# Rests of q and k of batches 3 to 5 subtracted on GpSimd instead of VectorE

## The reference, cut to what matters

```python
xn = layernorm(x)                                  # x is (8, 256, 128)
Q = rope(heads(xn, Wq)); K = rope(heads(xn, Wk)); V = heads(xn, Wv)     # 16 heads of 8
def attend(q, k):
    s = (q @ k.T + 0.1 * (q*q) @ (k*k).T) / sqrt(8)
    s = where(causal, s, -1e9)
    return softmax(s) @ V
out1 = attend(Q, K); out2 = attend(rotate_half(Q), rotate_half(K))      # equal scores
out = 0.5 * (out1 + out2) + 0.05 * (out1 * out2) * gate_w
x = x + out @ Wo.T
x = x + ffn0(layernorm(x)); x = x + attention1(layernorm(x)); x = x + ffn1(layernorm(x))
```

## Time and profile before

| | us |
|---|---|
| median of 3 runs | 329.7 |
| lowest and highest run | 328.73 and 331.28 |
| the profiled execution | 328.89 |
| its span in the profile | 326.9 |

### The profile page before, as it was taken

The page is one execution under the profiler, slowest core; times in us unless marked ns, Lnnn a source line. Parts: engine busy times, 40 slices in busy tenths (PEclk is TensorE's granted clock), DMA queues, the critical chain, the costliest instruction groups (busy, mean ns, idle before and its releaser), DMA issues.

```text
span 326.9 us, 8438 instructions
## 1 busy us (share of the span) xinstructions
PE 292.8 (90%) x2852; PEld 208.5 (64%) x2852; DVE 252.1 (77%) x1000; ACT 216.8 (66%) x494; POOL 176.5 (54%) x406
## 2 busy tenths in 40 slices
PE   7749779698999899999999999999999999999946
PEld 4526456466667676767776676766666665655625
DVE  7877979777878877677768677679798989895453
ACT  7661675566477768586767768597778777676711
POOL 5641674876774877777687614435453627170210
PEclk9976999999999999999999999999999999999996
DMA  6976214311213122221201110010211110100000
GB/s 198 323 169 156 65 54 113 115 49 39 80 49 117 52 65 66 52 82 38 71 23 53 36 58 27 24 59 27 69 31 60 41 42 28 42 4 19 18 8 24
DMA packets 23178, 21.59 MB, mean 66 GB/s; under 512 B 2944, under 2 KB 20096, under 8 KB 23136
## 3 DMA queue, kind: packets, MB, share of 16 engines
q1 hardware_dynamic: 23136, 21.05, 22.2%
HBM read 13.18 MB, written 7.34 MB: 63 GB/s over the span
## 4 chain that ended last, share of the span: by engine, by line
PE 55%; DVE 22%; POOL 9%; issue 7%; ACT 6%; POOLq 0%; ACTq 0%; DVEq 0%
PE bank L978 12%; DVE NM L757 7%; PE bank L1008 5%; PE bank L952 5%; PE bank L1021 5%; PE bank L928 3%; PE bank L929 3%; POOL XN L430 2%; PE bank L1067 2%; PE bank L956 2%; PE bank L926 2%; PE bank L889 2%; PE bank L1053 2%; ACT PB L590 2%; PE bank L875 2%
## 5 line engine op out<-in xcount | busy, mean ns | idle before, releaser
L590 ACT ACTIVATE PB<-bank 128x384 f32<-128x384 f32 (+1 forms) x256 | 134.8, 545 | 56.6 <-PE bank L954 31.9
L757 DVE TENSOR_REDUCE NM<-bank 128x2 f32<-128x512 f32 x128 | 83.9, 684 | 22.6 <-PE bank L929 22.2
L952 PE MATMUL bank<-QS,KS 128*128 128x256 f16 x256 | 69.8, 274 | 2.1 <-ACT PB L590 1.4
L978 PE MATMUL bank<-PB,VP 128*32 128x256 f32 (+1 forms) x1024 | 61.7, 358 | 2.5 <-POOL PB L469 1.7
L752 DVE CUSTOM_DVE_ANT_0 JUNK<-bank,MSF 128x128 bf16<-128x128 f32 x128 | 36.4, 285 | 24.5 <-PE bank L926 24.0
L754 DVE CUSTOM_DVE_ANT_0 JUNK<-bank,MSF 128x256 bf16<-128x256 f32 x128 | 53.7, 419 | 0.0
L978 PEld LDWEIGHTS bank<-PB,VP 128*32 128x32 f32 x1024 | 26.7, 109 | 25.6 <-issue 9.3
L469 POOL TENSOR_SCALAR_AFFINE_SELECT PB<-PB 128x512 f32<-128x512 f32 x64 | 41.1, 643 | 0.0
L926 PE MATMUL bank<-KS,QS 96*128 96x256 f16 x128 | 36.1, 285 | 0.0
L928 PE MATMUL bank<-KS,QS 96*128 96x256 f16 x128 | 35.2, 275 | 0.4
L929 PE MATMUL bank<-KS,QS 96*128 96x256 f16 x128 | 34.6, 271 | 0.0
(11 more groups left out here) (101 smaller groups left out, 608.1 us busy)
## 6 DMA issues: line engine op xcount, KB each, us to landing
scr<-PR SPq DMA_DIRECT2D x16, 256.0 KB, 2.8
QS<-scr SPq DMA_DIRECT2D x16, 128.0 KB, 2.6
QS<-scr SPq DMA_DIRECT2D x32, 64.0 KB, 2.8
KS<-scr SPq DMA_DIRECT2D x32, 64.0 KB, 2.8
KS<-scr SPq DMA_DIRECT2D x16, 128.0 KB, 3.0
scr<-PR SPq DMA_DIRECT2D x16, 128.0 KB, 1.9
out_x<-xs SPq DMA_DIRECT2D x8, 128.0 KB, 1.9
W<-in_w SPq DMA_DIRECT2D x1, 576.0 KB, 6.2
```

What stands on the lines that cost most here:

```text
L590: act.activation(PB[:, s % RING, 0:n], scored(i, s)[:, 0:n], ACT.Exp).then_inc(s_e, 1)
L757: dve.tensor_reduce(m[:, s, 0:2], o[:, :].rearrange("q (n k) -> q n k", n=2), AX.X, ALU.max, negate=True).then_inc(s_mx, 1)
L952: pe.matmul(o[:, 0:S], k[:, 0:P], q[:, :], start=True, stop=True)
L978: ins = pe.matmul(o, v, pr, start=(g % 2 == 0 and kt == 0), stop=True, skip_group_check=True)
```

## The change

The two `low` subtractions of batches 3, 4 and 5 move from DVE to POOL. They keep their slots. On each engine the tables are followed in the same way, so the place within the slot follows from the place of the code in the engine's loop: on POOL the slot begins with the `cut` (odd slots), goes on with the vectors of the other steps and the value spread (`spread_v`, slot 8), and the new `low_pool` comes behind these. No semaphore is added or removed: `low_pool` waits for `high` as `low` did and counts up the same semaphore.

```diff
+POOL_LOW = (3, 4, 5)
...
+            def low_pool(b, n):
+
+                p = b % 2
+                pool.wait_ge(s_hi, 2 * b + n + 1)
+                pool.tensor_tensor(PR[p][:, n, 2:4], QR[p][:, n], PR[p][:, n, 0:2], ALU.subtract).then_inc(s_lo, 1)
...
                         for n, step in enumerate(("rot_q", "rot_k")):
                             if a[step] == H * i + s:
                                 rotate(b, n)
+                        if a["lo"] == H * i + s and b in POOL_LOW:
+                            for n in range(2):
+                                low_pool(b, n)
...
-                        if a["lo"] == H * i + s:
+                        if a["lo"] == H * i + s and b not in POOL_LOW:
                             for n in range(2):
                                 low(b, n)
```

## The result

| | kernel before | changed kernel |
|---|---|---|
| median | 330.52 us (20 runs) | 328.12 us (20 runs) |
| lowest and highest | 327.67 to 331.72 | 326.51 to 330.09 |
| ratio, with 95% interval | | 0.9938 (0.9915 to 0.9962) |
| profiled execution, its span | 328.89, 326.9 | 329.68, 328.0 |

The ratio compares the fast runs alone, so it is not exactly the quotient of the medians. The changed kernel is faster by about 2 us; the interval leaves 0.8 to 2.8. The two profiled executions say the opposite: the changed kernel's is 0.8 us longer. So the first thing to learn is how far one profiled execution speaks for its kernel.

A forecast was written before the change was run, and what follows sets the result against it. PE is busiest at 90%, but the chain also runs through DVE's batch 3 pair and POOL's order of work. 0.58 + 0 − 0.59 = −0.01 us on 328.89, plus 0.8 for the median: 329.7 us, range 328.0 to 331.6.

The forecast's parts named there:

- The chain account of the phases: Waits from 30 to 63 us: batch 3 costs 0.58 us, batch 4 nothing, batch 5 gains 0.59.
- POOL's instruction: Each moved subtraction takes 1.156 us on POOL, as the same one in layer 1; 2.31 us for a pair.
- Batch 3's place: Phase 0, slot 1: POOL's new pair delays the cut of slot 3, so `pv` group 0 starts 0.58 us late.
- the XN of batch 6: POOL's normalised rows at 60.53 in phase 1: without DVE's pair alongside, 0.89 us in place of 1.48.
- the sum at `pv` group 1 of phase 1: All three batches' effects together, 0.58 + 0 − 0.59: −0.01 us, with the `pv` at about 62.8.
- Batch 4 costs nothing: Phase 0, slot 14: POOL's pair delays no one; `pv` group 3 has 1.0 us to spare.
- the third rival: POOL's new pair holds up DVE through the shared port pair; cost over 0.5 us, chance 0.03.
- The fourth rival: PE's longer stop at 39.2 to 40.2 lowers the granted clock: 4 us more, 333.7 median, chance 0.04.
- an offset that both kernels share: The runs' median is 0.8 us above the profiled execution, added to 328.9 to forecast 329.7 us.
- The second rival: Batch 3 costs nothing and batch 5's gain stays: −0.6 to −1.0 us, 328.7 to 329.1 median, chance 0.13.
- A chance of 0.92 for within 1%: Whole kernel: chance 0.92 that the time changes by no more than about 1%, 3.3 us, either way.

The follow-up runs named there:

- second measurement: The changed kernel timed again with the same edit, batches 3, 4 and 5 on POOL, against the kernel before: median 328.39 us, ratio 0.9940.
- filled version: Changed kernel plus 5, 2, 5 and 4 useless PE matmuls in slot 0, before `pv` group 0, slot 13, before `pv` group 1: 327.87 us, ratio 0.9958.
- the filled kernel before: Kernel before plus 5, 5 and 6 useless PE matmuls in slot 0, slot 13 and ahead of `pv` group 1 of phase 1: 327.91 us, ratio 0.9952.

## Why the prediction was wrong

- **The chain account of the phases was right.** POOL's instruction took 1.156 us as taken over from L513. Batch 3's place cost 0.43 us (forecast 0.58), the XN of batch 6 took 0.88 (forecast 0.89), and the sum at `pv` group 1 of phase 1 was −0.19 us (forecast −0.01), most of the difference being batch 3's 0.15. The profiles of the changed kernel's second measurement and of its filled version give −0.12 and −0.18 there.
- **Batch 4 costs nothing: right.** Alone it measures 1.0013 (0.9977 to 1.0049), and in the changed kernel `pv` group 3 doesn't wait (55.31, with no stop). ACT's instructions are 1.7 us later than in the kernel before's profile both at 45 and at 60 us, so neither the pair nor SP's later stores cost anything between.
- **DVE is held up by POOL too, as the third rival had it.** DVE's scaling of the gate took 0.60 us beside POOL's pair, where it was 0.21, and nothing came of it. The line of DVE in the changed kernel:

```profile
38.98 0.60 DVE L854 TENSOR_SCALAR SM<-SM 128x128 f32<-128x128 f32 x1
```

- **The step that failed is the clock.** The sum had no term for falls of the granted clock that the kernel before already has. The fourth rival said that a longer stop of PE might let the clock fall, gave it 0.04, and dismissed it because the page "shows a clock of 0.9 or more through the slice with the 1.69 us stop". That was one execution; behind the same stop the clock fell in two other profiles. So I had the mechanism, but with the wrong sign, at the wrong stop and too large: I looked for a fall behind the new stop ahead of `pv` group 0, where none of the three profiles with that stop unfilled shows one (1.29 or 1.30 us), and priced it at 4 us where a fall costs 1.1 to 1.3. The falls come with the stops that the change shortens: 1.69 to 1.08 us for the cut of slot 7, and those for batch 4's XN and the maxima at the head of phase 0.
- **The gap was in sight.** The profiled execution of the kernel before lay 0.8 us under the median, and the runs spread over 2.6 us. I carried the 0.8 over as an offset that both kernels share. It mixed executions with and without falls, beside the chance of the start and the end, and the share of falls is what the change altered. The term that was missing from the sum is about −1.8 us by the measured −2.0 less the account's −0.2, and −1.6 us by the filled kernel before (ratio 0.9952); both intervals are some 1 us wide on each side. The mean clock accounts for about 1 of the 1.8.
- The measured median of 328.12 lies inside my range of 328.0 to 331.6, but only at its edge, and the direction was missed. The second rival had the direction and a chance of 0.13, but not the reason: it wanted batch 3 to cost nothing, and it cost 0.43 us. A chance of 0.92 for within 1% was right.

What stays open: which stop brings the clock down in which execution. With the same stops, two profiles of the kernel before show none, batch 4 alone two, batches 4 and 5 one (at 37 us), batch 3 alone one (at 63 us). With eight profiles of the unfilled kernels the share for each place can't be given; the mean clock of the runs doesn't tell places apart. It isn't settled either how much of the gain belongs to the first place, where the change removes DVE's pair from the head of phase 0 and puts a stop of 1.29 us behind it. No run fills the stops of one place with a fill that fits, so the two places were not tried apart.

## What to carry to other kernels

A profile in which the clock stays up behind a stop does not show that it always does: read the mean clock of each timed run beside its time, and where the two go together, take several profiles and look at the clock behind PE's stops. There a small saving on another engine can be worth more than its own size (here 0.2 us by the waits, and about 2 us in the runs), and a handful of idle matmuls that fit into the stops can bring as much. And when two profiled executions are compared, take out the difference of their starts first; here it was 1.3 us, more than the change itself in the trace.

## What the runs showed of the hardware

- TensorE's clock fell to half behind a stop of 1.7 us in two executions and stayed up behind the same stop in two others. A fall cost 1.1 to 1.3 us, by four falls in three profiles.
- VectorE and GpSimd stretch each other on tensors in SBUF. Beside VectorE's pair, which has two inputs there, XN took 1.48 in place of 0.88 us and the value spread 1.44 in place of 0.52, and the pair itself 1.84 in place of 1.29. Beside GpSimd's pair the tiny scaling on VectorE took 0.60 in place of 0.21. The Trainium skill's "SBUF — State Buffer", section "SBUF: two separate sides", states this as an exclusive lock, for VectorE with two SBUF inputs or in a two-port mode; the rows agree, and for the scaling no run shows the mode.
- A subtraction of two SBUF tensors, 128 × 512 with a float16 result, takes 1.156 us on GpSimd and 0.692 on VectorE, a factor of 1.67. The Trainium skill's "GPSIMD Engine Reference", section "Engine selection", has about 2 for work with two inputs; for this shape the measured 1.67 decides.
